# A graph network kernel: the norms' scale and bias products on two row groups of TensorE's array

## What is computed

```python
def _cond_layer_norm(x, cond, sw, sb, bw, bb):
    mu = jnp.mean(x, axis=-1, keepdims=True)
    var = jnp.var(x, axis=-1, keepdims=True)
    xn = (x - mu) * jax.lax.rsqrt(var + EPS)
    scale = cond @ sw + sb
    bias = cond @ bw + bb
    return xn * (1.0 + scale) + bias
```

## Time and profile before

| | |
|---|---|
| median of 3 runs | 1870.88 us (1868.85 to 1871.59) |
| the profiled execution | 1871.84 us, of which its span is 1870.1 us |
| granted TensorE clock over the span | 0.996 of 2.4 GHz |
| PE busy | 1810.0 us, 97% of the span |
| PEld busy (weight loads) | 1575.5 us, 84% |
| DVE busy | 1382.6 us, 74% |
| ACT busy | 826.5 us, 44% |
| POOL busy | 453.8 us, 24% |
| bytes moved | 108.43 MB, 58 GB/s |

### The profile page before, as it was taken

How to read it: one execution, slowest core, us unless ns; L and a number is a source line. 1 busy time by engine, 2 the same in 40 slices (tenths; PEclk the granted TensorE clock), 3 DMA queues, 4 the chain that set the end, 5 groups by cost and what they waited for, 6 DMA issues and landing times. The chain is left out here.

```text
span 1870.1 us, 33910 instructions
## 1 busy us (share of the span) xinstructions
PE 1810.0 (97%) x11814; PEld 1575.5 (84%) x11814; DVE 1382.6 (74%) x2847; ACT 826.5 (44%) x1613; POOL 453.8 (24%) x547
## 2 busy tenths in 40 slices
PE   6988999999999999999999999999999999999999
PEld 4656988999789889998898899988998999887877
DVE  8996668888875588888754988888549888885431
ACT  1552465555432255554322545544226545536220
POOL 2000333112341341113413411125134111262000
PEclk9999999999999999999999999999999999999999
DMA  4213462110300111113011211040112110522001
GB/s 143 55 41 79 141 176 91 38 43 27 123 24 34 58 42 39 38 31 124 4 54 42 58 38 38 27 128 1 46 50 61 38 38 27 142 72 55 1 1 55
DMA packets 50755, 108.43 MB, mean 58 GB/s; under 512 B 18170, under 2 KB 18222, under 8 KB 50640
## 3 DMA queue, kind: packets, MB, share of 16 engines
q1 hardware_dynamic: 50608, 106.87, 19.7%
q0 software_dynamic: 32, 0.03, 0.0%
HBM read 83.62 MB, written 23.25 MB: 57 GB/s over the span
## 5 line engine op out<-in xcount | busy, mean ns | idle before, releaser
L876 ACT ACTIVATE PT<-ps 125x500 fp32r<-125x500 f32 (+1 forms) x480 | 214.3, 520 | 315.1 <-PE ps L1790 315.1
L1690 PE MATMUL ps<-PT,V 125*128 125x250 f32 x2400 | 313.2, 284 | 1.7 <-DVE PT L1288 1.7
L1690 PE MATMUL ps<-kT,qg 128*125 128x512 f32 (+1 forms) x1440 | 302.1, 354 | 6.3 <-DVE nmx L1272 5.6
L1690 PEld LDWEIGHTS ps<-kT,qg 128*125 128x125 f32 x1440 | 245.4, 186 | 56.0 <-issue 6.9
L1690 PEld LDWEIGHTS ps<-PT,V 125*128 125x128 f32 x2400 | 289.6, 190 | 2.9 <-DVE PT L1288 2.9
L1288 DVE TENSOR_TENSOR PT<-ps,PT 125x500 fp32r<-125x500 f32 (+1 forms) x480 | 253.1, 582 | 2.1 <-ACT PT L876 1.7
L1272 DVE CUSTOM_DVE_ANT_0 SB<-ps,bt 125x1250 f32<-125x1250 f32 x140 | 203.9, 1457 | 47.4 <-PE ps L1690 44.6
L1790 PE MATMUL ps<-ident,pbuf 125*125 125x125 f32 x1600 | 202.2, 273 | 9.9 <-DVE PT L1288 4.0
L1790 PEld LDWEIGHTS ps<-ident,pbuf 125*125 125x125 f32 x1600 | 187.2, 189 | 13.6 <-issue 8.8
L870 ACT ACTIVATE pbuf<-SB,nmx 125x1250 f32<-125x1250 f32 x140 | 188.1, 1344 | 12.1 <-DVE nmx L1272 10.4
L1281 DVE TENSOR_SCALAR pbuf<-pbuf,rden 125x1250 f32<-125x1250 f32 x160 | 150.1, 938 | 5.6
(11 more groups left out here) (246 smaller groups left out, 2811.6 us busy)
## 6 DMA issues: line engine op xcount, KB each, us to landing
bt<-edge_bias_scratch SPq DMA_DIRECT2D x40, 546.9 KB
q_scratch<-qc SPq DMA_DIRECT2D x16, 500.0 KB, 2.6
qc<-q_scratch SPq DMA_DIRECT2D x16, 500.0 KB, 4.8
counts_scratch<-cblk SPq DMA_DIRECT2D x10, 546.9 KB
c_rows<-counts_scratch SPq DMA_DIRECT2D x10, 546.9 KB
edge_bias_scratch<-b_rows SPq DMA_DIRECT2D x10, 546.9 KB
counts<-counts_scratch SPq DMA_DIRECT2D x10, 546.9 KB
wm<-in_L_gnn_wo_dram SPq DMA_DIRECT2D x4, 1024.0 KB, 8.6
```

The lines of the kernel that those rows point to most:

```text
L876: sc.activation(PT[:, h % 2, 0, a:b, u * T:(u + 1) * T], ps_T[0:T, i, 0:(b - a) * T].rearrange("p (t n) -> p t n", n=T), ACT.Copy).then_in ...
L1690: e = mm(out_, lhs(a), rhs(b), start=start and i == 0, stop=stop and i == 2)
```

## The change

`lnw`, `lnS`, `condS` and `condc` get 115 partitions (`KC = 64 + 51`) in place of 96, in two groups of 51 rows, from partition 0 for the scale and from partition 64 for the bias. [...] Each of the four matmuls of `scale_bias` contracts over the 51 rows of its group: the scale over partitions 0 to 50, the bias over partitions 64 to 114. The order of the four and their waits stay.

`load_ln` issues 14 loads in place of 12. `split_ln` copies 512 columns in place of 1024, and subtracts twice over 512 columns in place of once over 1024. DVE's first split is two operations of half the size. The low part of `cond` goes to a tile of its own, `condL`, and six copies by DMA, issued by SP after the store of the eighth count tile, fill the rest of `condS`; POOL's first `cond_chunk` waits for them.

```diff
-KC = 96
+KR = 3 * (C + 1)
+KC = 64 + KR
...
+        condL = place("condL", [C + 1, N], F32R, r_yT2)
...
             def load_ln(l, sw, sbias, bw, bbias):
-                for q in (0, 32, 64):
-                    sp.dma_start(lnw[q:q + C, 0, :], lay(sw, l)).then_inc(s["ldLN"], 16)
-                    sp.dma_start(lnw[q + C:q + C + 1, 0, :], row(sbias, l)).then_inc(s["ldLN"], 16)
-                    sp.dma_start(lnw[q:q + C, 1, :], lay(bw, l)).then_inc(s["ldLN"], 16)
-                    sp.dma_start(lnw[q + C:q + C + 1, 1, :], row(bbias, l)).then_inc(s["ldLN"], 16)
+                for q, w, b in ((0, sw, sbias), (64, bw, bbias)):
+                    for r in (0, 32):
+                        sp.dma_start(lnw[q + r:q + r + C, 0, :], lay(w, l)).then_inc(s["ldLN"], 16)
+                        sp.dma_start(lnw[q + r + C:q + r + C + 1, 0, :], row(b, l)).then_inc(s["ldLN"], 16)
+                    sp.dma_start(lnw[q + C + 1:q + 2 * C, 0, :], lay(w, l)[0:C - 1, :]).then_inc(s["ldLN"], 16)
+                    sp.dma_start(lnw[q + 32 + C + 1:q + 32 + C + 2, 0, :], lay(w, l)[C - 1:C, :]).then_inc(s["ldLN"], 16)
+                    sp.dma_start(lnw[q + 32 + C + 2:q + KR, 0, :], row(b, l)).then_inc(s["ldLN"], 16)
...
             for t in range(NT):
+                if t == NT - 2:
+                    sp.wait_ge(s["condL"], 1)
+                    for to, of in ((condS[C + 1:2 * C, :], condL[0:C - 1, :]), (condS[32 + C + 1:KR, :], condL[C - 1:C + 1, :]),
+                                   (condS[64:64 + C + 1, :], condS[0:C + 1, :]), (condS[64 + C + 1:64 + 2 * C, :], condL[0:C - 1, :]),
+                                   (condS[96:96 + C + 1, :], condS[32:32 + C + 1, :]), (condS[96 + C + 1:KC, :], condL[C - 1:C + 1, :])):
+                        sp.dma_start(to.bitcast(F32), of.bitcast(F32)).then_inc(s["condS"], 16)
...
             def split_ln(i):
...
-                g.tensor_copy(lnS[:, :, :], lnw[:, :, :]).then_inc(s["lnhi"], 1)
+                g.tensor_copy(lnS[:, 0, :], lnw[:, 0, :]).then_inc(s["lnhi"], 1)
...
-                q = slice(32, 32 + C + 1)
-                g.tensor_tensor(lnS[q, :, :], lnw[q, :, :], lnS[q, :, :].bitcast(F32), ALU.subtract).then_inc(s["lnS"], 1)
+                for r in (32, 96):
+                    q = slice(r, r + C + 1)
+                    e = g.tensor_tensor(lnS[q, 0, :], lnw[q, 0, :], lnS[q, 0, :].bitcast(F32), ALU.subtract)
+                e.then_inc(s["lnS"], 1)
...
-            pool.wait_ge(s["condS"], 1)
+            pool.wait_ge(s["condS"], 16 * 6)
             cond_chunk(0, PROJECTED[0])
...
                 dve.wait_ge(s["condS0"], 1)
-                v.tensor_tensor(condS[64:64 + C + 1, :], condT[:, :], condS[0:C + 1, :].bitcast(F32), ALU.subtract).then_inc(s["condS"], 1)
+                v.tensor_tensor(condL[:, :], condT[:, :], condS[0:C + 1, :].bitcast(F32), ALU.subtract).then_inc(s["condL"], 1)
...
-                        e = mm(ps_sb[:, u, a, :], condc[:, u * T:(u + 1) * T], lnS[:, a, :], start=True, stop=True)
+                        e = mm(ps_sb[:, u, a, :], condc[64 * a:64 * a + KR, u * T:(u + 1) * T], lnS[64 * a:64 * a + KR, 0, :], start=True, stop=True)
```

More of the change, by code:

```diff
@@ L271, in build @@
                      "h1 cond_mm condT rm rel cand cand_t red red_t tab prefix tabi onehot0 onehot1 oh_used0 oh_used1 ct_mm ct ct_t ct_e "
-                     "i_sum i_sq i_st c_ld0 c_ld1 bln bmask bdone bst_out0 bst_out1 cnt_out0 cnt_out1 condS0 condS lnhi lnS onesr "
+                     "i_sum i_sq i_st c_ld0 c_ld1 bln bmask bdone bst_out0 bst_out1 cnt_out0 cnt_out1 condS0 condL condS lnhi lnS onesr "
                      "bn stats lnv r0 nw xn sb ysc y yTp yT condc "
@@ L511, in split_ln @@
             def split_ln(i):
-                pool.wait_ge(s["ldLN"], 192 * (i + 1))
+                pool.wait_ge(s["ldLN"], 224 * (i + 1))
                 pool.wait_ge(s["sb"], AHEAD + NC * i)
                 settled(pool)
-                g.tensor_copy(lnS[:, :, :], lnw[:, :, :]).then_inc(s["lnhi"], 1)
+                g.tensor_copy(lnS[:, 0, :], lnw[:, 0, :]).then_inc(s["lnhi"], 1)
                 pool.wait_ge(s["lnhi"], i + 1)
                 settled(pool)
-                q = slice(32, 32 + C + 1)
-                g.tensor_tensor(lnS[q, :, :], lnw[q, :, :], lnS[q, :, :].bitcast(F32), ALU.subtract).then_inc(s["lnS"], 1)
+                for r in (32, 96):
+                    q = slice(r, r + C + 1)
+                    e = g.tensor_tensor(lnS[q, 0, :], lnw[q, 0, :], lnS[q, 0, :].bitcast(F32), ALU.subtract)
+                e.then_inc(s["lnS"], 1)
                 pool.wait_ge(s["lnS"], i + 1)
@@ L527, in cond_chunk @@
                 g.tensor_copy(condc[:, :], condS[:, bass.ds(c * W, W)].bitcast(F32)).then_inc(s["condc"], 1)
-            pool.wait_ge(s["ldLN"], 192)
-            g.tensor_copy(lnS[:, :, :], lnw[:, :, :]).then_inc(s["lnhi"], 1)
-            pool.wait_ge(s["condS"], 1)
+            pool.wait_ge(s["ldLN"], 224)
+            g.tensor_copy(lnS[:, 0, :], lnw[:, 0, :]).then_inc(s["lnhi"], 1)
+            pool.wait_ge(s["condS"], 16 * 6)
             cond_chunk(0, PROJECTED[0])
@@ L1156, in first_ln_low @@
                 dve.wait_ge(s["lnhi"], 1)
-                q = slice(32, 32 + C + 1)
-                v.tensor_tensor(lnS[q, :, :], lnw[q, :, :], lnS[q, :, :].bitcast(F32), ALU.subtract).then_inc(s["lnS"], 1)
+                for r in (32, 96):
+                    q = slice(r, r + C + 1)
+                    e = v.tensor_tensor(lnS[q, 0, :], lnw[q, 0, :], lnS[q, 0, :].bitcast(F32), ALU.subtract)
+                e.then_inc(s["lnS"], 1)
             def split_wa_lo(i):
```

## The result

The changed kernel takes 1873.89 us (median of 20 runs, 1870.54 to 1877.09) against 1870.76 us for the kernel before in the same measurement (20 runs, 1868.85 to 1871.60): ratio 1.0017, 95% interval 1.0010 to 1.0023. It is 3.1 us slower, within the 0.2% that I called no change, and 2.4 us over the forecast of 1871.5. The profiled execution of after took 1873.33 us with a span of 1871.8; that of before 1871.84 and 1870.1.

A forecast was written before the change was run, and what follows sets the result against it. PE's stream was taken to bound the kernel. Calls +0.5 us and DVE's split +0.1 gave +0.6 on the profiled 1871.84, so 1872.4, or 1871.5 us against the median 1870.88; range 1860 to 1878.

The forecast's parts named there:

- the 0.2% that I called no change: Whole kernel: a measurement can tell about 0.2%, 3.7 us, from no change; chance of same 0.53, faster 0.20, slower 0.27.
- my own forecast's bounds: Whole kernel: forecast with its bounds, 1868.7 to 1873 us, chance 0.53.
- the +0.6 us: Whole kernel: +0.5 us from the calls and +0.1 us from DVE's first split.
- The drains: PE, into and out of each call: changing between 51 and 128 rows costs 0.40 us a call, bounds 0 and 0.56.
- The saving: PE, each call: scale and bias run side by side, two of four steps go, 0.475 us, less lag 0.375 us.
- the lag: PE, first pair of a call: the second matmul starts up to 0.10 us late, as two loads step 0.10 us apart.
- loads side by side: PE, each call: loads of two row groups overlap, net -0.08 us a call, -2.1 us in sum.
- Which calls count: Of 40 calls in `project`, attention's end and `mlp`, a loss counts 30 times and a gain 22 times.
- Rival (2): 30 calls: array drains twice a call but scale and bias run one after the other; +12, 1883 us; chance 0.13.
- Attention's end: End of attention, 4 calls: PE idles for DVE, so the change costs and brings nothing; without that cover 0.03 us.
- The six copies: Start: six issues of 0.35 us, landing at most 4.8 us, end near 161.3; 3 us of cover before 165.20.
- The split and the loads: Norms, SP and POOL: last load 0.7 us later, copy -0.5, subtractions 2.4 to 2.6; `condc` at 469.1, 4.4 us cover.

The follow-up runs named there:

- experiment 7: Changed kernel, but all four matmuls of a call read rows 0 to 50, so scale and bias share a row group; 1881.05 us, ratio 1.0057.
- experiment 6: Kernel before, with one of four matmuls left out at attention's end and the other three contracting over 65 rows; 1876.18 us, ratio 1.0030.
- experiments 2: Changed kernel, but the four calls at attention's end use all 115 rows (old form), the other 36 stay paired; 1870.79 us, ratio 1.0001.
- Experiment 1: Changed kernel, but all 40 calls in the old form over all 115 rows, new loads, copies and split kept; 1872.84 us, ratio 1.0011.
- 9: Three kernels (36 calls paired; repeated matmuls at attention's end; all calls old form), each with copies one tile earlier; 1868.20, 1867.46, 1870.88 us.
- 4: Changed kernel plus four repeated matmuls (two pairs) ahead of the fourth matmul at attention's end; 1869.82 us, ratio 0.9999.
- 3: Changed kernel, but only the four calls at attention's end paired, the other 36 in the old form over 115 rows; 1875.05 us, ratio 1.0025.
- Experiments 8: Changed kernel, with its six copies alone issued one tile earlier; 1871.52 us, ratio 1.0009.
- 9's first: Changed kernel, but attention's end calls in the old form over 115 rows and the six copies one tile earlier; 1868.20 us, ratio 0.9990.
- experiment 5: Kernel before, with one of the four matmuls left out at attention's end, old form kept; 1870.54 us, ratio 0.9998.
- Experiment 1 with early copies: Changed kernel, but all 40 calls in the old form over 115 rows and the copies one tile earlier; 1870.88 us, ratio 1.0006.

## Why the prediction was right or wrong

The time lies in the range and on the side of no change that got the largest chance. That was in part luck: the measured time is 0.9 us past the 1873 to which my own forecast's bounds reached, and of the terms of the +0.6 us two were mis-sized and one was missing, and they partly cancel.

**The drains: right.** In `project` of the changed kernel the first of the four starts 0.20 us behind the last 250-column matmul, as said, and the product behind has a bare load with the weight loader idle for "issue". 51 rows are on the side of 42, not on that of 96. All of it together can be read from experiment 7, which drains but doesn't pair: its call takes 1.12 us where the earlier trace rows has 0.95, 0.17 more; with the start at 0.20 and not at 0.11 and the bare load behind it comes to about 0.36 us (chunks 18.89 us apart against 18.54), where I had 0.40. The Trainium skill, "TensorEngine Tiling (Array Packing)", Key Properties, says that changing the mode drains the engine. The trace agrees, also for 51 rows in fp32r; experiment 6 with 65 rows shows no drain.

**The saving: right in size, wrong in the lag.** I had taken 0.10 us off because two loads step 0.10 us apart. That step failed. The four loads keep the loader busy for 0.30 us, where the earlier trace rows has 0.78, and scale and bias of a tile start 3 ns apart (at 596.76 us 0.203 and 0.206 us behind the last 250-column matmul). Two full steps go: 0.46 us by experiment 7. The Trainium skill, "TensorE: Matmul & The Clock Gate", Part 3, gives about 4 ns for a further tile, and the trace agrees with 3. The value that I had named beside mine, loads side by side, holds: -0.09 us a chunk in `project` against -0.08. The sum that belongs to it, -2.1 us, is what the 36 pairs bring in experiments 2 against 1 (-1.9) and in 9 (-3.0).

**Which calls count: partly wrong.** `project` carries it in full. In `mlp` I let chunks 1 and 2 pass on a loss, through POOL's wait for `sb`, and chunk 0 too. Experiment 7 gives them a loss of 0.46 us, and the steps stay at 13.37 us; behind chunk 0 nothing is passed on either. What sets these steps isn't shown (DVE, the next candidate, is busy 11.6 of 13.4 us there). As the net was no loss, this cost the forecast nothing. Rival (2) with its 30 calls was priced at 1883 us, and experiment 7, which is this rival in the flesh, came to 1881; but falls of the clock are in that number, so their nearness is partly chance.

**Attention's end: the step that failed.** "The change costs and brings nothing" is true of the work: the fourth matmul starts 1.53 us after the start of the last turn in both kernels. It is false of the clock. I costed idle time at nothing because DVE hides it, and took the clock before and after as the same. The four matmuls span 51 rows in place of 96 amid two waits for DVE, and in three of four blocks the clock then fell to 1.2 GHz and cost some 1.5 us. It is 2.6 to 3.6 us in all (after against 2 and 4, 3 against 1, 8 against 9's first), as much as the whole difference in time.

The Trainium skill, "TensorE: Matmul & The Clock Gate", Part 1, has the gate follow how busy PE has been. Here the measurement adds to it: experiment 5 is less busy than the changed kernel and keeps its clock, experiment 6 with equal records and fewer rows loses it.

**The six copies: mis-sized.** I had them end at 161.3; they ended at 165.85. The issues took 5.9 us (154.33 to 160.25) and not 2.1, as an issue took 0.6 to 1.5 us and not 0.35, and the landing took 5.6 us and not 4.8. The point at which it costs was stated rightly ("5 us later, 2 us would be lost, once"): 4.5 us late, PE started 1.1 us late. But where the clock doesn't fall the second call starts no later for it, and what I hadn't priced is that the clock often falls behind that wait. Experiments 8 and 9 put the start at 0.9 to 2.2 us.

**The split and the loads: right.** The `condc` of a norm is ready at 469.83 (469.43 + 0.40), I had 469.1; this execution runs 0.63 us behind the one before at that place, by the call of the earlier trace rows (474.14 against 473.51). The two subtractions take 2.63 us, just past my 2.6:

```profile
464.04 0.25 SPq L339 DMA_DIRECT2D lnw<-in_L_gnn_b_b_dram  x1
...
465.74 0.61 POOL L526 CAST lnS<-lnw 115x512 fp32r<-115x512 f32 x1 [6.85 <-DMA lnw<-in_L_gnn_b_b_dram]
466.53 2.63 POOL L531 TENSOR_TENSOR lnS<-lnw,lnS 17x512 fp32r<-17x512 f32 x2 [0.18 <-POOL lnS L526]
469.43 0.40 POOL L539 CAST condc<-condS 115x250 fp32r<-115x250 f32 x1 [0.26 <-POOL lnS L531]
```

**The sum as it stands now**: pairs -1.9 to -3.0, attention's end +2.6 to +3.6, start +0.9 to +2.2; with the middles -2.4 + 3.1 + 1.6 = +2.3 us, against 3.1 measured. The rest is inside the uncertainty. Experiment 1 with early copies, 1.0006 (0.9996 to 1.0015), leaves between nothing and 2.8 us for the rest of the change.

## What to carry to other kernels

Two matmuls on disjoint row groups of 51 rows run side by side and save a whole step, but each change between such a group and the full array costs about 0.18 us of drain and bare load; a pair of pairs amid full-array work just pays for that, so pack only where several pairs stand together or PE has nothing else near. Where PE waits for another engine, a cheaper matmul isn't free: look at the granted clock of the stretch behind it, and try the form over many rows there (here it was worth 2.6 to 3.6 us for four calls). Price small copies between partitions by their issues as well, and put them as early as their source allows: here one tile earlier was worth some 1 to 2 us.

## What the runs showed of the hardware that I had not expected

- The granted clock depended on the rows of the matmuls, at equal records and equal idle time: three matmuls over 96 rows and no fall at four ends, three over 65 rows and falls at two of four, with 6 us by the ratios and a mean clock of 0.9927 against 0.9958.
- Loads of two row groups start 3 ns apart in fp32r, where loads to the full array step 0.10 us.
- Six copies of 2 to 17 rows from partition to partition took 5.9 us of SP's time to issue and 5.6 us more to land; an issue took 0.6 to 1.5 us, that of a norm's load from memory 0.23 to 0.33 (but for one of 2.7).
- Why the clock falls in some blocks of an execution and not in others isn't settled: at attention's end it fell in 12 of 20 cases, with the same work ahead of it each time.
